# A graph network's edge loop: target rows and weight remainders in one tile, a subtraction moved to GpSimd, single-tile loops for rare cases

## What is computed

```python
h = maximum(layernorm(x), 0)
messages = mlp3(concat([h[src], h[dst], edges]), mW1, mb1, mW2, mb2, mW3, mb3)
summed = segment_sum(messages, src) + segment_sum(messages, dst)
paired = h.reshape(-1, 2, 32, 128); attention = the difference within each pair
x = x + mlp3(concat([h, summed, attention]), uW1, ..., ub3)
h = maximum(layernorm(x), 0)
# graph convolution: self loops, degrees counted over dst
x = x + gelu(D^-1/2 (C + I) D^-1/2 (h @ W) + b)      # C counts edges per (dst, src)
```

## Time and profile before

| | |
|---|---|
| Median of 3 runs | 844.16 us (842.46 to 846.85) |
| The profiled execution | 844.42 us; its span is 842.7 us |
| TensorE busy (matmul) | 799.7 us, 95% |
| VectorE busy | 649.9 us, 77% |
| ScalarE busy | 511.9 us, 61% |
| GpSimd busy | 308.4 us, 37% |
| Chain that ended last | TensorE 91%, VectorE 6% |

### The profile page before, as it was taken

How to read it: one execution, slowest core, us unless ns; L and a number is a source line. 1 busy time by engine, 2 the same in 40 slices (tenths; PEclk the granted TensorE clock), 3 DMA queues, 4 the chain that set the end, 5 groups by cost and what they waited for, 6 DMA issues and landing times.

```text
span 842.7 us, 14028 instructions
## 1 busy us (share of the span) xinstructions
PE 799.7 (95%) x4396; PEld 631.2 (75%) x4396; DVE 649.9 (77%) x1478; ACT 511.9 (61%) x708; POOL 308.4 (37%) x349
## 2 busy tenths in 40 slices
PE   4579999999999999999999999999999999997797
PEld 4447778777777887777887777778777778875567
DVE  6988888877778887878887777888787788757344
ACT  2227666677666667666666766666676666665231
POOL 2526433344333344443334444333444433350100
PEclk9769999999999999999999999999999999998799
DMA  7523323322332332232233222233323223220000
GB/s 205 167 69 108 95 84 92 94 85 78 88 87 90 92 92 82 88 90 84 86 95 91 83 83 86 88 88 95 89 79 94 85 85 88 76 74 15 2 0 26
DMA packets 42778, 71.12 MB, mean 84 GB/s; under 512 B 10192, under 2 KB 22032, under 8 KB 42704
## 3 DMA queue, kind: packets, MB, share of 16 engines
q1 hardware_dynamic: 30032, 35.61, 14.4%
q0 software_dynamic: 12672, 34.62, 14.2%
HBM read 66.52 MB, written 3.67 MB: 83 GB/s over the span
## 4 chain that ended last, share of the span: by engine, by line
PE 91%; DVE 6%; issue 1%; ACT 1%; DVEq 1%; DMA 0%; ACTq 0%
PE bank L693 29%; PE bank L672 21%; PE bank L682 13%; PE bank L623 8%; PE bank L615 6%; PE bank L703 4%; PE bank L611 4%; PE bank L826 2%; PE bank L785 1%; DVE oh_key L1146 1%; DMA x_sb<-x 0%; PE bank L793 0%; PE bank L779 0%; DVE oh_low L1145 0%; DVE h_lo L1055 0%
## 5 line engine op out<-in xcount | busy, mean ns | idle before, releaser
L886 ACT ACTIVATE dist<-iota_h,neg_mid 128x1024 f16<-128x1024 f16 x256 | 293.0, 1146 | 8.4 <-DVE inc L1078 8.4
L479 POOL DMA_INDIRECT tab_all<-table_a,ends_i x252 | 256.2, 1017 | 67.5 <-issue 67.5
L1078 DVE TENSOR_SCALAR inc<-dist,half_gap,times 128x1024 fp32r<-128x1024 f16 x252 | 205.0, 815 | 47.6 <-ACT dist L886 47.4
L879 ACT ACTIVATE h_sb<-bank,b_sb 128x512 f32<-128x512 f32 x128 | 87.5, 683 | 171.7 <-PE bank L672 171.7
L693 PE MATMUL bank<-inc,m_hi 128*128 128x512 f32 x512 | 173.1, 420 | 6.2 <-DVE inc L1078 4.6
L693 PE MATMUL bank<-inc,m_lo 128*128 128x512 f32 x512 | 161.9, 398 | 0.0
L489 POOL CAST near_w<-near_raw 128x256 fp32r<-128x256 f32 x63 | 29.0, 460 | 353.4 <-DMA near_raw<-table_bl 353.4
L1062 DVE SCALAR_TENSOR_TENSOR h_lo<-bank,h_hi 128x512 fp32r<-128x512 f32 x128 | 87.8, 686 | 86.0 <-ACT h_hi L873 84.6
L1146 DVE TENSOR_SCALAR oh_key<-iota_h,key_f,minus_base 128x258 bf16<-128x258 f16 x330 | 132.1, 400 | 0.0
L682 PE MATMUL bank<-w_sb,h_sb 128*128 128x128 f32 x1024 | 125.0, 275 | 0.8 <-ACT h_sb L879 0.8
L873 ACT ACTIVATE h_hi<-bank 128x512 fp32r<-128x512 f32 x126 | 75.3, 598 | 80.6 <-PE bank L619 80.2
(11 more groups left out here) (197 smaller groups left out, 807.4 us busy)
## 6 DMA issues: line engine op xcount, KB each, us to landing
e_raw<-edge_attr_t SPq DMA_DIRECT2D x128, 128.0 KB, 2.7
dst_all<-dst_row SPq DMA_DIRECT2D x63, 128.0 KB, 3.0
tab_all<-table_a,ends_i POOLq DMA_INDIRECT x252, 2.8
near_raw<-table_bh SPq DMA_DIRECT2D x63, 32.0 KB, 1.8
near_raw<-table_bl SPq DMA_DIRECT2D x63, 32.0 KB, 1.7
table_a<-tab_all SPq DMA_DIRECT2D x1, 1024.0 KB, 4.9
table_bh<-h_hi SPq DMA_DIRECT2D x4, 256.0 KB, 3.6
table_bl<-h_lo SPq DMA_DIRECT2D x4, 256.0 KB, 3.4
```

What stands on the lines that cost most here:

```text
L479: nc.gpsimd.indirect_dma_start(to, None, table, bass.IndirectOffsetOnAxis(ap=ends, axis=0)).then_inc(done, 16)
L879: nc.scalar.activation(h2_sb[:, m, :], z2_bank[m][:, :], ACT.Relu, bias=b2_sb[:, m:m + 1]).then_inc(h2_ready, 1)
L886: nc.scalar.activation(dist[:, t, :], iota_h[:, :], ACT.Abs, bias=neg_mid[:, bass.ds(tile, 1)]).then_inc(dist_ready, 1)
L1078: nc.vector.tensor_scalar(inc[:, t, :], dist[:, t, :], half_gap[:, tile], times[:, tile], ALU.is_equal, ALU.mult).then_inc(inc_ready, 1)
```

## The change

- **One full-height tile.** `near_hot` gets the rounded edges in partitions 0 to 63 (a second copy by ScalarE in `split_edges`), so that target-row runs and the remainder of W1e are one matmul per bank over 128 partitions. `half_in` goes; the first layer of g+1 is one piece, and all four tiles of g-1 are scattered behind the messages of g.
- **Messages.** VectorE adds the bias b3 to the messages into a new tile `m_sb`, which has one buffer (`sum_messages`); ScalarE rounds that; GpSimd subtracts (`low_messages`), for groups 0 to 61; VectorE does so for 62 and 63. The bias matmuls at the end go.
- **GpSimd's order.** In iteration g behind the four gathers: low_messages(g-5), then the wait for near load g and the cast.
- **SyncE's order.** Near load g+2 is issued with edges and targets of g+2, all behind `e_ready` g+1; near loads 0 and 1 go ahead of the loop.
- **All 64 groups are main groups.** The far loop visits single tiles; its forced visit is the last tile. General window visits are by single tiles too, their window and tile worked out on VectorE in each visit, after the edge loop, beside the update network. Windows are made in the step of their own number; none is made ahead.
- **Start.** Ends are turned and spread first on TensorE; base rows are worked out earlier; `list_more` goes; the weights for the split are loaded first and split earlier; steps -2 and -1 of the loop run between the preparations.

Core of the diff (the run-time loops and the preparations are left out; their content is told above):

```diff
-    MAIN = GROUPS - 1
+    MAIN = GROUPS
     RING = 4
+    HERE = MAIN - 2
...
-            for g in range(MAIN):
-                load_near(g)
-                if g + 2 < MAIN:
-
-                    sp.wait_ge(e_ready, g + 1)
-                    load_edges(g + 2, g % 2)
-                    load_targets(g + 2, g % 2)
+            load_near(0)
+            load_near(1)
+            for g in range(MAIN - 2):
+
+                sp.wait_ge(e_ready, g + 1)
+                load_edges(g + 2, g % 2)
+                load_targets(g + 2, g % 2)
+                load_near(g + 2)
...
+            def low_messages(g):
+
+                pool.wait_ge(m_hi_ready, g + 1)
+                nc.gpsimd.tensor_tensor(m_lo[:, g % 2, :, :], m_sb[:, :, :], m_hi[:, g % 2, :, :].bitcast(F32),
+                                        ALU.subtract).then_inc(m_lo_ready, 1)
+
             for g in range(MAIN):
                 b = g % RING
                 if g >= RING:
...
                     gather_rows(got[:, b, t, :], table_a, ends_i[:, 0, tile:tile + 1], ga_done[b][t])
+                if g > RING:
+                    low_messages(g - RING - 1)
                 pool.wait_ge(near_loaded[g % 2], 32 * (g // 2 + 1))
                 nc.gpsimd.tensor_copy(near_w[:, g % WINS, :], near_raw[:, g % 2, :]).then_inc(near_ready, 1)
-
-            pool.wait_ge(near_ready, MAIN)
+            for g in range(MAIN - RING - 1, HERE):
+                low_messages(g)
...
+            def near_part(b, slot):
+
+                for k in range(KH):
+                    nc.tensor.matmul(z1t_bank[k][:, :], near_w[:, slot, k * P:(k + 1) * P], near_hot[:, b, :],
+                                     start=False, stop=False, skip_group_check=True)
...
+            def first_layer(g):
+
+                pe.wait_ge(e_ready, g + 1)
+                wait(pe, h1_lo_ready, 2 * g)
+                edge_part(g % 2)
+                pe.wait_ge(near_ready, g + 1)
+                near_part(g % 2, g % WINS)
+                for k in range(KH):
+                    for t in range(GT):
+                        if k == 0:
+                            pe.wait_ge(ga_done[g % RING][t], 16 * (g // RING + 1))
+                        mm = turn_rows(g % RING, t, k)
+                    mm.then_inc(z1t_psum, 1)
...
-                wait(pe, m_lo_ready, g)
+                wait(pe, m_ready, g)
...
-                if nxt:
-                    first_layer(g + 1, 0)
-                if past and not more:
-                    scatter(g - 1, 1 - b, 0)
-                if nxt:
-                    first_layer(g + 1, 1)
-                if now and not more:
-                    messages(g)
-                if b == 1 and summed_in(i):
-                    window(i + 1)
+                if nxt:
+                    first_layer(g + 1)
+                if now:
                     messages(g)
+                if b == 0 and i > 0:
+                    window(i - 1)
                 if past:
-                    scatter(g - 1, 1 - b, 1)
-                    scatter(g - 1, 1 - b, 2)
-                    scatter(g - 1, 1 - b, 3)
+                    for t in range(GT):
+                        scatter(g - 1, 1 - b, t)
...
             def split_edges(b):
 
-                nc.scalar.copy(e_hl[:, b, :], e_raw[:, b, :]).then_inc(e_cast, 1)
+                nc.scalar.copy(e_hl[:, b, :], e_raw[:, b, :])
+                nc.scalar.copy(near_hot[0:ED, b, :], e_raw[0:ED, b, :]).then_inc(e_cast, 1)
...
+            def sum_messages(g):
+
+                dve.wait_ge(m_psum, g + 1)
+                wait(dve, m_lo_ready, g)
+                nc.vector.tensor_tensor(m_sb[:, :, :], msg_bank[:, :].rearrange("p (t d) -> p t d", t=GT),
+                                        b3_all[:, :].unsqueeze(1).broadcast_to([P, GT, D]), ALU.add).then_inc(m_ready, 1)
...
                 if now:
+                    sum_messages(g)
                     incidence(g, 0)
+                if HERE <= g < MAIN:
                     low_messages(g, b)
```

More of the change, by code:

```diff
@@ L400, in _ @@
                 load_targets(g, g)
+            for to, frm in loads:
+                sp.dma_start(to, frm).then_inc(ld_w, 16)
             sp.wait_ge(tab_a_ready, NC // 2)
@@ L527, in spread_ends @@
                         col = end_mm[:, half, which:which + 1].broadcast_to([P, P])
[L528 removed]
+                        mm = nc.tensor.matmul(bank[7][:, (2 * which + half) * P:(2 * which + half + 1) * P], col,
                                               ident[:, :], start=(which == 0 and half == 0), stop=True,
@@ L573, in table_rows @@
                     mm.then_inc(tab_psum, 1)
-            for c in range(NC):
-                table_rows(0, c)
-            turn_ends()
-            for c in range(NC):
-                table_rows(1, c)
-            spread_ends()
+            for which in range(2):
+                for c in range(NC):
+                    table_rows(which, c)
             def update_of_node(k):
@@ L647, in far_group, with far_tile @@
+            def far_tile(v):
                 g = v + MAIN
+                one = slice(0, P)
                 pe.wait_ge(e_ready, g + 1)
                 pe.wait_ge(h1_lo_ready, 2 * g)
-                edge_part(1)
-                low_part(1, 0, 0)
-                low_part(1, 0, 1)
+                for k in range(KH):
+                    part = slice(k * P, (k + 1) * P)
+                    nc.tensor.matmul(z1t_bank[k][:, one], w1e_hi[:, part], e_hl[:, 0, one], start=True, stop=False,
+                                     skip_group_check=True)
+                    nc.tensor.matmul(z1t_bank[k][:, one], near_w[0:ED, 0, part], near_hot[0:ED, 0, one], start=False,
+                                     stop=False, skip_group_check=True)
@@ new lines, in far_tile @@
+                parts = [(w, a, k) for w, a in ((w2_hi, h1_hi), (w2_lo, h1_hi), (w2_hi, h1_lo)) for k in range(KH)]
+                for m in range(KH):
+                    for n, (w, a, k) in enumerate(parts):
+                        mm = nc.tensor.matmul(z2_bank[m][:, one], w[:, k, m * P:(m + 1) * P], a[:, 0, k, one],
+                                              start=(n == 0), stop=(n == len(parts) - 1))
+                    mm.then_inc(z2_psum, 1)
+                pe.wait_ge(h2_ready, 2 * g + 2)
@@ new lines, in far_tile @@
+                for k in range(KH):
+                    mm = nc.tensor.matmul(msg_bank[:, 0:D], h2_sb[:, k, one], w3_sb[:, k, :], start=(k == 0),
+                                          stop=(k == KH - 1), skip_group_check=True)
+                mm.then_inc(m_psum, 1)
+                pe.wait_ge(m_lo_ready, g + 1)
+                for part in (m_hi, m_lo):
+                    for n in range(NH):
+                        mm = nc.tensor.matmul(acc_bank[n][:, :], part[:, 0, 0, :], inc[:, 0, n * HB:(n + 1) * HB],
+                                              start=False, stop=(part is m_lo), skip_group_check=True)
@@ L851, in _ @@
                 nc.scalar.activation(h_hi[:, n * HB:(n + 1) * HB], bank[n][:, :], ACT.Relu).then_inc(h_hi_ready, 1)
+            act.wait_ge(u_node_ready, 2)
+            for k in range(W1_SPLITS, len(splits)):
+                high_weight(k)
             for pair in range(NC // 2):
```

503 lines of the change are left out of this document (224 added, 279 removed).

## The result

| | before | after |
|---|---|---|
| Median | 845.28 us (842.46 to 846.85, 4 runs) | 945.53 us (932.78 to 949.95, 4 runs) |
| Ratio to before | | 1.1097 (95% interval 1.0984 to 1.121) |
| Profiled execution, its span | 844.42, 842.7 | 942.54, 940.8 |
| TensorE, VectorE, GpSimd busy | 95%, 77%, 37% | 84%, 74%, 43% |

The change makes the kernel 11% slower. The prediction was 939 us, in a range of 858 to 965. Medians are of all executions, while a ratio compares fast executions alone: it leaves out those over 1.5% above the fastest of their kernel, here two of the changed kernel's four (948.52 and 949.95 us) and, further down, one of e9's six (1088.36 us at a mean granted clock of 0.65).

A forecast was written before the change was run, and what follows sets the result against it. TensorE bounds the old loop; afterwards its wait for GpSimd's late subtraction closes a loop of T = 26.8 us per two groups. Front 62, 29 T, last groups 51 and the remaining end terms make 162 + 29 T = 939 us, range 858 to 965.

The forecast's parts named there:

- What bounds the loop, and the count of groups: Edge loop: TensorE's scatter waits 3.3 us for GpSimd's subtraction, low_messages(g) standing in iteration g+5, in every second group.
- The rival that ends faster: Edge loop: the subtraction comes in time, TensorE bounds two groups at 21.14 us, 775 us in all; chance 0.15.
- T = 26.8: Edge loop: time of two groups in us, 24.5 from the chain of waits plus 2.3 for the clock.
- Cast to the end of the fourth gather: GpSimd in the loop: from the near_w cast through four gathers, 5.54 us by the earlier trace's mean.
- The clock: TensorE behind most waits: half clock, costing 2.3 us per two groups.
- The other three links: Edge loop: first layer's end to low_edges' end 4.1 us, low_edges to cast 5.0, subtraction with hops 1.5.
- the second rival's 872: Edge loop: late subtraction but the clock stays full, two groups take 24.5 us, 872 us in all; chance 0.22.
- these two cases: Edge loop: late subtraction, with half clock (939 us, chance 0.60) or with full clock (872 us, chance 0.22).
- The front: Start of the kernel: GpSimd's 24 gathers, five casts and the subtraction bring the first scatter to 62 us.
- The end: After the last late scatter: last groups 51 us, far tile 7, copy 0.7, update 38.4, window visit 1.3.
- The sum: Whole kernel: 162 + 29 T, with 26.8 us for two groups, gives 939 us.
- What would show it: Trace signs: some 30 scatter waits of 3 us, cast waiting for DMA, clock below 1, TensorE 80 to 86%.

The follow-up runs named there:

- e9: e1's kernel with the gathers of groups 2 and 3 held until groups 0 and 1 passed the first layer; 776.68 us, ratio 0.9185.
- e1: The changed kernel with VectorE making the remainder of the messages in every group, GpSimd in none; 788.82 us, ratio 0.9257.
- e2: The changed kernel with GpSimd's subtraction ahead of the four gathers of its iteration instead of behind them; 792.34 us, ratio 0.9299.
- e3: The changed kernel with near load g+2 issued ahead of SyncE's wait for e_ready g+1; 790.07 us, ratio 0.9279.
- e4: The changed kernel with 14 extra matmuls nobody reads where TensorE waits, in odd groups 3 to 59; 920.65 us, ratio 1.0785.
- e5: The changed kernel with GpSimd's subtraction after the second of the four gathers instead of the fourth; 853.80 us, ratio 1.0082.

## Why the prediction was right, and where it was off

- **What bounds the loop, and the count of groups.** Right. The chain through low_edges g+2, near load g+4, cast g+4, gathers g+5 and the subtraction of g is the one in the rows above, and each of three cuts removes it (e1, e2, e3). TensorE's own work for two groups was put at 21.14; without a wait it is 21.11. The rival that ends faster needed the subtraction 3.3 us earlier; its time of 775 would have been right had that been so (e9: 776.68; e1 with the stall 788.82).
- **T = 26.8.** Measured 26.62 in the mean and 26.72 in the period shown. Two of its terms were off in opposite senses. *Cast to the end of the fourth gather*: 5.54 by the earlier trace rows, 6.57 measured, three gathers of 1.25 to 1.49 instead of 0.95. *The clock*: 2.3, the mean of the two stretches of the earlier trace rows; 1.67 measured in this period, next to the lower of them, and 1.5 in the mean, since in four periods it costs nothing. The other three links came 0.43 lower together (4.04, 4.80 and 1.33 for 4.1, 5.0 and 1.5). That these errors cancel in T is luck.
- **So the second rival's 872 was wrong.** With a full clock the quiet T is 25.25, not 24.5, and e4 took 920.65. The prediction's mechanism had 0.82 in these two cases together; how it split the loss between the chain and the clock did not hold.
- **The place from which the error came.** The gathers' durations were taken from a loop in which their operations and VectorE's fell otherwise in time. In the changed kernel's period each of the long gathers begins inside one of VectorE's `inc` operations (last section). The prediction cited the lock for the subtraction alone, which it hardly lengthened (62 of them, 1.28 us in the median, 1.46 at most), and put nothing on the gathers or on VectorE's operations in the chain.
- **The front.** First late scatter forecast at 62, measured at 67.52. GpSimd's casts and gathers were counted back to back from the earlier trace rows; it then waited 5.61 us for near load 0 ahead of its first cast. The term was short by that wait: each instruction of a queue counts, and so do its DMA waits.
- **The end.** From the last late scatter (839.63) to the end of the span 101.2, forecast 98.4. The last groups took 50.2 (51), the far tile with the copy of the sums 8.5 (7.7), and the rest 42.5 (39.7). The far tile's price and the window visit's held; of the 2.8 over, 2.2 is the update's first product, 5.88 us where the earlier trace rows has 3.65.
- **The sum.** 67.5 + 29 x 26.62 + 101.2 = 940.8; forecast 62 + 777.2 + 98.4. Errors of +5.5, -5.1 and +2.8 partly cancel, so the closeness of 939 to 942.5 for this execution (945.53 for the median) is in part luck; the mechanism is not.
- **What would show it.** 32 waits of 3.5 us in the mean (forecast some 30 of 3), the cast still waiting for its DMA, clock below 1, TensorE at 84% (80 to 86), full-height matmuls 0.23 apart (408.67 to 409.13 holds two).

## What to carry to other kernels

Before an operation moves to an idle engine, write down what stands in that engine's queue in front of it, and follow each of those instructions to what it waits for; if the chain ends at the engine that will wait for the moved operation, its length is the new period, however idle the engine looks. Such a loop can be opened at any link, and the cheapest was one line on SyncE: issue a load ahead of a wait that it doesn't need. When one link is shortened, look at what its instructions now run beside: e5's earlier subtraction lengthened another link by 1 us. When experiments put a number on one part (the clock), take that part away alone and leave the wait; the sum of two parts can be right with neither of them right.

## What the runs showed of the hardware

**The subtraction on GpSimd takes its time from VectorE.** VectorE's first one-hot of a tile, by kernel (busy us, mean ns): e1, which subtracts on VectorE, and the changed kernel:

```profile
L1146 DVE TENSOR_SCALAR oh_low<-iota_h,low_f 128x128 bf16<-128x128 f16 x321 | 82.2, 256 | 12.5 <-issue 5.6
```

```profile
L1150 DVE TENSOR_SCALAR oh_low<-iota_h,low_f 128x128 bf16<-128x128 f16 x321 | 121.3, 378 | 10.8 <-issue 7.2
```

One instance beside the subtraction at 414.79 to 416.06:

```profile
414.58 1.54 DVE L1150 TENSOR_SCALAR oh_low<-iota_h,low_f 128x128 bf16<-128x128 f16 x1
```

0.25 us of work took 1.54 and ended with the subtraction, which kept its own 1.27. `inc` grew from 0.81 to 2.13 in the same way at 398.13. Moving 43 us of subtraction off VectorE (62 of the 64 of 689 ns in e1) thus made it only 9 us less busy: 676.3 us in e1, 667.3 in e3.

**The reverse for gathers.** VectorE's `inc` operations beside the four gathers above:

```profile
408.35 0.82 DVE L1069 TENSOR_SCALAR inc<-dist,half_gap,times 128x1024 fp32r<-128x1024 f16 x1
...
410.19 0.81 DVE L1069 TENSOR_SCALAR inc<-dist,half_gap,times 128x1024 fp32r<-128x1024 f16 x1
...
411.90 0.81 DVE L1069 TENSOR_SCALAR inc<-dist,half_gap,times 128x1024 fp32r<-128x1024 f16 x1 [0.31 <-ACT dist L862]
```

The gathers at 408.77, 410.32 and 412.11 begin with 0.40, 0.68 and 0.60 us of an `inc` still to run, and are 0.30, 0.54 and 0.46 longer than 0.95; the one at 413.83 meets none and takes 0.95. From 100 us on, 86 gathers of the changed kernel begin inside an `inc` and take 1.35 us in the median; the other 141 take 0.95. The Trainium skill, page "SBUF — State Buffer", section "SBUF: two separate sides", describes both: the pair of ports is locked for a whole instruction, and a DMA issued from GpSimd is held up while VectorE has them. The rows of the gathers agree with it. Those of the subtraction agree that one side stands while the other runs, but not that an instruction keeps the ports once it has begun: the one-hot's record begins 0.21 us and that of `inc` 0.29 us ahead of the subtraction's, and both were stretched by 1.3 us while the subtraction kept its length.

**Where the clock falls, the time scatters.** The kernel before stays within 0.5% over four runs, the changed one within 1.8%, and with the wait filled it is 0.7% (915.54 to 921.62). Most waits of 3.7 us are followed by the lower clock, four of the periods by none, and how much full work then runs at the lower level differs: 5 us after 416.12, 3 us after 389.40. That this makes the scatter is likely, not shown: the fastest of the changed kernel's executions (932.78 us) has a mean clock of 0.927, the next (942.54) 0.931. e5's waits, 1.9 us at most between 100 and 700 us, leave its clock there at 0.99.
